# A diffusion layer and a deformable convolution on one core: five edits in the first image's chain, a new order of work, and 11 instead of 8 taps fetched by SyncE

## The reference

```python
x = x + L0(gn(x))      # gn: group norm, 32 groups of 2 channels
x = x + L1(gn(x))

# L0: two gates g, g1 = relu(bn(dwconv3x3(h))), Sobel gradients gx, gy, then 5 steps:
Dx, Dy = 1/(gy*gy/4 + 1), 1/(gx*gx/4 + 1)
D = 1/(1 + 2*Bx + 2*By);  c0 = 1 - 2*Bx - 2*By       # Bx, By = Dx*DT, Dy*DT
for _ in range(5):
    prev = h
    h = D*(c0*h0 - 2*E*h + cm_x*roll(h,1,2) + cp_x*roll(h,-1,2) + cm_y*roll(h,1,3) + cp_y*roll(h,-1,3))
    h = h + D*(2*DT)*x;  h0 = prev
return relu(bn(h))

# L1: deformable 3x3 convolution
offsets_y, offsets_x, mask = split(conv3x3(x, w_offset) + b_offset)   # 9 taps each
sampled = bilinear(x, y0 + offsets_y, x0 + offsets_x) * sigmoid(mask) # 4 corners of each tap
out = einsum(sampled, filt)
```

## Time and profile before

| | |
|---|---|
| median of three runs | 807.94 us (807.9 to 808.3) |
| the profiled execution | 803.14 us, its span 801.3 us |
| PE busy | 669.2 us (84%), mean granted clock 0.904 |
| DVE busy | 539.4 us (67%) |
| ACT busy | 242.2 us (30%) |
| POOL busy | 544.0 us (68%), of it 568 gathers 538.7 us |
| the chain that ended last | POOL 57%, issue 20%, PE 12%, DVE 7% |

### The profile page before, as it was taken

The page is one execution under the profiler, slowest core; times in us unless marked ns, Lnnn a source line. Parts: engine busy times, 40 slices in busy tenths (PEclk is TensorE's granted clock), DMA queues, the critical chain, the costliest instruction groups (busy, mean ns, idle before and its releaser), DMA issues.

```text
span 801.3 us, 15341 instructions
## 1 busy us (share of the span) xinstructions
PE 669.2 (84%) x4616; PEld 589.9 (74%) x4616; DVE 539.4 (67%) x906; ACT 242.2 (30%) x469; POOL 544.0 (68%) x583
## 2 busy tenths in 40 slices
PE   8976888899899988989799987999799987655656
PEld 6865667788788888768689887778778877544545
DVE  5695479778977896578866895778866796322122
ACT  4414421542145213522144313522154213000000
POOL 2000777777777777777777777777777777777774
PEclk9997988999999999999989998999899998555557
DMA  5102333533353433543353435343353335333432
GB/s 167 56 3 55 97 110 109 159 108 115 109 166 109 128 110 112 163 122 109 109 167 114 121 110 167 107 126 108 113 162 114 109 108 167 111 109 108 114 111 72
DMA packets 55146, 92.80 MB, mean 116 GB/s; under 512 B 13384, under 2 KB 35480, under 8 KB 55064
## 3 DMA queue, kind: packets, MB, share of 16 engines
q0 software_dynamic: 27264, 74.49, 31.9%
q1 hardware_dynamic: 27608, 17.20, 7.7%
q10 hardware_dynamic: 192, 0.15, 0.1%
HBM read 79.37 MB, written 12.40 MB: 115 GB/s over the span
## 4 chain that ended last, share of the span: by engine, by line
POOL 57%; issue 20%; PE 12%; DVE 7%; ACT 2%; DMA 1%; POOLq 0%; SPq 0%; DVEq 0%; ACTq 0%
POOL pixels L558 57%; PE banks L1150 9%; PE banks L1153 4%; DVE weighted L903 1%; DMA pixels<-table,index 1%; DVE banks L759 1%; DVE prod L778 0%; DVE prod L798 0%; DVE row_squares L582 0%; ACT coef_T L1051 0%; DVE prod L816 0%; DVE prod L779 0%; ACT sampled_T L1063 0%; DVE banks L760 0%; DMA taps<-taps_in 0%
## 5 line engine op out<-in xcount | busy, mean ns | idle before, releaser
L558 POOL DMA_INDIRECT pixels<-table,index x568 | 538.7, 948 | 247.6 <-issue 172.4
L1153 PE MATMUL banks<-const,weighted 128*128 128x128 f32 x1280 | 194.5, 308 | 62.8 <-DVE weighted L903 49.5
L903 DVE TENSOR_TENSOR weighted<-pixels,banks 128x2304 f32<-128x2304 f32 (+1 forms) x65 | 161.2, 2480 | 115.7 <-DMA pixels<-table,index 111.8
L1153 PEld LDWEIGHTS banks<-const,weighted 128*128 128x128 f32 x1280 | 169.6, 163 | 73.9 <-DVE weighted L903 53.8
L1063 ACT ACTIVATE sampled_T<-banks 128x512 f32<-128x512 f32 (+1 forms) x128 | 55.7, 435 | 335.1 <-PE banks L1153 334.3
L1153 PE MATMUL banks<-const,prod 128*128 128x128 f32 x816 | 109.9, 278 | 19.3 <-DVE prod L778 12.9
L1153 PEld LDWEIGHTS banks<-const,prod 128*128 128x128 f32 x816 | 90.7, 143 | 28.2 <-DVE banks L760 14.1
L1150 PE MATMUL banks<-conv_w,xT 128*128 128x64 f32 (+2 forms) x576 | 97.7, 325 | 0.7 <-ACT banks L1040 0.7
L1150 PEld LDWEIGHTS banks<-conv_w,xT 128*128 128x128 f32 x576 | 91.4, 191 | 7.0 <-ACT banks L1040 1.6
L1150 PE MATMUL banks<-filt,sampled_T 128*128 128x64 f32 x640 | 87.0, 286 | 7.2 <-ACT sampled_T L1063 7.2
L1150 PEld LDWEIGHTS banks<-filt,sampled_T 128*128 128x128 f32 x640 | 81.5, 202 | 13.5 <-ACT sampled_T L1063 11.5
(11 more groups left out here) (144 smaller groups left out, 651.6 us busy)
## 6 DMA issues: line engine op xcount, KB each, us to landing
far_pixels<-table SPq DMA_DIRECT2D x1024, 1.0 KB
pixels<-table,index POOLq DMA_INDIRECT x568, 2.7
table<-xn SPq DMA_DIRECT2D x48, 128.0 KB
table<-xn SPq DMA_DIRECT2D x16, 144.0 KB
x<-x_in SPq DMA_DIRECT2D x30, 64.0 KB, 2.6
out_dram<-x SPq DMA_DIRECT2D x60, 32.0 KB
table<-corner_w SPq DMA_DIRECT2D x16, 70.0 KB
const<-const_in SPq DMA_DIRECT2D x2, 384.0 KB, 3.9
```

The lines of the kernel that those rows point to most:

```text
L558: pool.indirect_dma_start(out=pixels[:, col % NB, k, :], out_offset=None, in_=table[0:(u + 1) * TY * TX, :], in_offset=bass.IndirectOffset ...
L903: return dve.tensor_tensor(weighted[:, col % 2, :, a:b, :].rearrange("p q k c -> p k q c"), entries.rearrange("p k (q c) -> p k q c", c=C) ...
L1153: return pe.matmul(dst, data, moved, start=start, stop=stop, is_transpose=True, skip_group_check=True)
```

## The change

- SyncE fetches 1, 1, 2, 1, 2, 1, 2, 1 taps of the images' last columns (`FAR_TAPS`, 11 in all) instead of one each; GpSimd gathers as many fewer (`gathered`). The addresses are made in bytes on VectorE (`far_addresses`), and the DMA takes them as an offset into the table seen as bytes. The first 32 fetches of an image stand where they stood, the others (96 or 224) in one run in the second half.
- The halo column is made by PE together with the turned edges and copied by VectorE within `edges2`; the table's write waits for that (`emptied(u, "edges2")`).
- The cell below a position is found by adding and subtracting a large constant (`ROUND`): two operations instead of four.
- ScalarE loads its function tables by set; `log` and `exp` share one set.
- In image 0 alone: h's first value is copied to PSUM by ScalarE (`init+0`) instead of being made by PE, into a bank that PE writes once ahead of it; the force of each step is added by PE (`stf1` to `stf4`, four transposes each) instead of VectorE; the gates' differences are split in two (`ownx`, `owny`), and they go to another bank.
- The orders of the three engines are new. At the start VectorE's is now `rows1+0 mean1+0 rows1+1 rowsq1+0 var1+0 bnpa+0 bnpb+0 bnpc+0 scale1+0 shw+0` (before: `rows1+0 mean1+0 bnpa+0 rowsq1+0 bnpb+0 var1+0 bnpc+0 shw+0 scale1+0`, and `rows1+1` after image 0's last step). In the later images the multiply of the fourth column (`mult@11`, `mult@19`, ...) stands behind `scale1` of the image after next instead of behind `rows2`.

```diff
-FAR_W, FAR_K = WS - 1, K2 - 1
-FAR_REGS, FAR_FIRST = 16, 32
-WARM_UP = (6, 4, 6)
+FAR_TAPS = (1, 1, 2, 1, 2, 1, 2, 1)
+FAR_W, FAR_MOST = WS - 1, max(FAR_TAPS)
+FAR_LOADED, FAR_FIRST = 16, 32
+WARM_UP = (6, 1, 6)
...
-rows1+0 mean1+0 bnpa+0 rowsq1+0 bnpb+0 var1+0 bnpc+0 shw+0 scale1+0 dif+0 cells+0 edges1+0 bnout+0 den+0 diff+0
+rows1+0 mean1+0 rows1+1 rowsq1+0 var1+0 bnpa+0 bnpb+0 bnpc+0 scale1+0 shw+0 dif+0 cells+0 edges1+0 bnout+0 den+0
...
             def write_table(u):
-                sp.wait_ge(*emptied(u, "halo"))
+                sp.wait_ge(*emptied(u, "edges2"))
...
-                for p in range(first, last, FAR_REGS):
-                    sp.load(regs, far_index[0:1, u % 2, p:p + FAR_REGS])
-                    for i in range(FAR_REGS):
-                        sp.dma_start(far_pixels[p + i:p + i + 1, u % 2, :], table[bass.ds(sp.snap(regs[i]), 1), :])\
-                          .then_inc(s_far[u], 16)
+                for n in range(first, last, FAR_LOADED):
+                    tap, p = divmod(n, P)
+                    _, at = nc.values_load_multi_w_load_instructions(
+                        far_at[tap:tap + 1, u % 2, p:p + FAR_LOADED], engines=(mybir.EngineType.SP,), min_val=0,
+                        max_val=(ENTRIES - 1) * 4 * ENTRY, skip_runtime_bounds_check_because="positions are clipped")
+                    for i in range(FAR_LOADED):
+                        sp.dma_start(far_pixels[p + i:p + i + 1, u % 2, tap, :].bitcast(u8),
+                                     table_bytes[bass.ds(at[i], 4 * ENTRY)]).then_inc(s_far[u], 16)
...
-                        fetch_far(u + 1, FAR_FIRST, P)
+                        fetch_far(u + 1, FAR_FIRST, FAR_TAPS[u + 1] * P)
...
         def gathered(col):
-            return K2 - 1 if col % WS == FAR_W else K2
+            return K2 - (FAR_TAPS[col // WS] if col % WS == FAR_W else 0)
...
                 for dh in ROW_ORDER:
+                    if what == "edges2" and dh == ROW_ORDER[-1]:
+                        dve.tensor_copy(xn2[:, WS + 1, :], bank(u, what)[:, 2 * P:2 * P + C])
...
                 dve.wait_ge(s_prod, 5 * n)
+                if u == 0:
+
+                    dve.tensor_tensor(target(m), (c0[:, :], c0_T)[1 - m % 2], target(m), ALU.mult).then_inc(s_seeded, 1)
+                    return
...
-                seq(dve.tensor_copy(pos_int[:, :], ps))
-                seq(dve.tensor_copy(lo, pos_int[:, :]))
-                seq(dve.tensor_tensor(ab, lo, ps, ALU.is_gt))
-                seq(dve.tensor_tensor(lo, lo, ab, ALU.subtract))
-                entry = ab[:, 0:WS * K2]
+
+                seq(dve.tensor_scalar(lo, ps, -0.5, ROUND, ALU.add, ALU.add))
+                seq(dve.tensor_scalar(lo, lo, -ROUND, None, ALU.add))
+                entry = entries[:, :]
...
-                    i = len(loaded) % UNUSED
-                    act.activation(unused[:, i:i + 1], one, after)
+                    act.preload_act_table_set(after)
...
+                elif name == "init":
+                    act.wait_ge(s_xn, 1)
+                    act.wait_ge(s_preset_bank, 1)
+                    act.activation(source(0), xn[:, :], ACT.Copy).then_inc(s_init, 1)
...
+            def first_force(m):
+                pe.wait_ge(s_seeded, m)
+                if m % 2:
+                    pe.wait_ge(*emptied(0, "tF"))
+                src = force_T if m % 2 else force[:, :]
+                for j in range(PAIRS):
+                    add(pair(target(m), PAIRS - 1 - j), pair(src, j), eye)
...
-                        mm(bank(0, "conv1"), ones[:, :], x1[0][:, :], True, True).then_inc(s_preset_bank, 1)
+                        for of_engine in (bank(0, "conv1"), source(0)):
+                            ins = mm(of_engine, ones[:, :], x1[0][:, :], True, True)
+                        ins.then_inc(s_preset_bank, 1)
                         warm_up(WARM_UP[1])
```

## The result

The changed kernel takes **849.15 us** (median of four runs, 844.5 to 853.3) against 807.92 of the kernel before: 1.052 times as long, 95% interval 1.049 to 1.055. The prediction was 824.0, with a range of 799 to 845. The direction and the mechanism came as forecast, the size did not: the time lies 4 us above the range.

A forecast was written before the change was run, and what follows sets the result against it. GpSimd's unbroken gathers bound the kernel; SyncE would become the bound at images 3, 5 and 7. Start +2.1, gathers -3.8 and stalls +18 sum to +16.3: 824 us by the median, range 799 to 845 (forecast's own 811 to 850).

The forecast's parts named there:

- The frame: Whole kernel: time is first gather's start, number of gathers and tail, plus GpSimd's standstill for a table or indices, zero before.
- The gathers: GpSimd: 565 gathers instead of 568, 1.253 us each, -3.8 us if GpSimd remains the bound.
- The room: Time from an even image's row numbers to the end of its 70 gathers: 113 us, against 124 us of SyncE's work.
- a lead of 27: Image 2's indices ahead of their first gather: 27 us, today's 19 to 22 with an estimated 6 for the moved multiply.
- the prediction's own formula: Stall at an odd image: SyncE's time to the next table's landing beyond the lead and 70 gathers; 11 us at image 3.
- The prediction's other sum, 43: Stalls at images 3, 5 and 7 if leads stay at today's 19 to 22 us: 16 + 16 + 11 us.
- The start: First gather 2.1 us later: +6.9 up to image 0's normalised x, -4.8 in the rest of its chain.
- a gain of 1.1 us: Image 0's indices come 1.1 us sooner: two index operations go and `turn+1` no longer stands ahead of `off+0`.
- The tail: Behind the last gather: code and cuts unchanged, so it stays at 10.2 us.
- Rival B: SyncE keeps up with a fetch near 0.27 us, the early wait costs as forecast: 806.3 us; chance 0.25.
- C: SyncE keeps up and the early wait for image 1's input costs nothing: 799.8 us; chance 0.15.
- D: SyncE's register operations save nothing, 0.427 us a fetch: each stall 20 us longer, 860 and more; chance 0.06.

The follow-up runs named there:

- another, with the changed kernel's order at that place: Changed kernel, 11 taps, with image 1's row sums moved behind image 0's first edge copies on VectorE: 1.052 of the kernel before, span 838.6 us.
- The old form of the fetch: Changed kernel, 11 taps, fetching by row numbers instead of byte positions, so one register operation more per fetch: 1.175 of the kernel before, span 943.6 us.
- the run without the wait: Changed kernel with image 1's row sums behind image 0's first edge copies: 1.052 of the kernel before with 11 taps, 0.998 with eight.
- eight taps: Changed kernel with SyncE fetching one tap in every image, 8 instead of 11: 1.006 of the kernel before, span 805.2 us.
- one double in image 2, in image 5: Two runs, changed kernel with a second tap in that image alone: image 2 1.036 of the kernel before, image 5 1.008.
- the warm one: Changed kernel with eight taps, image 1's row sums later and 33 unused ones products on PE: 0.991 of the kernel before, median 797.51 us.
- the warm kernel with both orders: The eight-tap kernel with row sums later and unused ones products, plus image 1's turn and first gradient back ahead on PE: 0.992 of the kernel before.

## Why the prediction was wrong in size and right in kind

**The frame held.** Three terms and a fourth, start, number and tail plus stalls, account for the span within 2 us. One fetch was put at 0.34 us and took 0.336; the register operation went, the MOVE stayed. From an even image's indices to the next table were to be 126 us (2 + 124) and were 124.0. The gathers were -3.8, at 1.253 each.

**The room was mis-sized, and this is the error**: +18 was forecast, 42.9 came.
- At image 3: a lead of 27 was assumed. It was 11.2. The 27 starts from image 4's lead of 22 and not from image 2's own 19, and adds 6 for the moved multiply. The 6 came from a row of an image in which that multiply waits for pixels; in the changed kernel none of the eleven multiplies that VectorE makes between 150 and 260 us waits for pixels (the longest wait ahead of one, 5.13 us, is for PE), so the move frees nothing in images 1 and 2. The lead then fell by 8 more, since image 1's chain became 8 us longer. The run that puts PE's work for image 1 back ahead shortens the stall by 5.0, but another, with the changed kernel's order at that place, reached as much, so the shares of order and clock are open. With a lead of 11.2 the prediction's own formula gives 126 - 11.2 - 87.7 = 27 against 24.9: the formula was sound and its input wrong. I had named a lead that I could not read as what spoke against the forecast, and still took it from a row of image 4.
- At images 5 and 7: 6 + 1 were forecast, 10.5 + 7.5 came. The leads of images 4 and 6 were indeed at the 32 that the prediction gave (31.5 both). But the prediction had SyncE begin an even image's fetches as soon as the row numbers are there. Image 4's indices were ready at 434.18, and SyncE, busy with image 3's fetches until 433.6, then with a store, image 4's table and its landing, began at 444.5 with the first register load. Once it has no idle time left, the stall is no longer a matter of leads but of two sums, 188.7 against 176.7 us a pair. The old form of the fetch shows the same: 224.7 a pair.
- The prediction's other sum, 43 "with today's leads", meets the measured 42.9 by luck: its parts are 16, 16 and 11, the measured ones 24.9, 10.5 and 7.5, and with image 2's own lead of 19 the first would have been 19.

**The start** was put at +2.1 and came at +4.2. x was normalised at 16.7 instead of 17.35. The early wait cost 5.1 us (2.9 of waiting, 1.9 of clock and a rest), where 3.6 and 1 had been set for it; the batch-norm steps took 1.85 as forecast (11.24 to 13.09 in the run without the wait). The 2 us missed fit the offsets: `turn+1` no longer ahead of `off+0` was booked as part of a gain of 1.1 us. It was what brought PE to the higher clock; without it the 36 products took 7.72 us instead of 4.91, as in every profile with neither the turn nor ones products ahead of them. The run with the turn ahead has its first gather 2.3 sooner. But the start is no fixed number: four profiled kernels with the same code up to there (changed, eight taps, one double in image 2, in image 5) have their first gather at 84.9, 83.1, 85.7 and 82.7, so +2.0 to +5.0, and the forecast of +2.1 lies at the lower end.

**The tail** was left at 10.2, as its code is unchanged, and took 12.9. The code is the same; the granted clock in it is not (last section).

**Rival B** (SyncE keeps up) and **C** (faster) needed a fetch of 0.27 us or x landing before 8 us; neither was so. **D** had the right sign and too low a price for the same reason as the forecast: it counted three stalls from leads, and not pairs.

## What to carry to other kernels

Before work is moved to an engine with "idle time", add up what that engine's queue does per period, and compare with the period of the engine that it feeds: as long as the sum is smaller, a delay costs only what exceeds the lead, and the lead has to be read at the very image where it is spent; once it is larger, every period costs the difference. A piece of work that looks free to move on TensorE may be what brings its clock up, a wait put into its way may lose it, and a chain of small products behind an idle stretch is priced by rows at both levels. Thirty-three products without a use, placed in waits, were worth more here (0.998 to 0.991) than the new order and all the edits with it (1 to 0.998).

## What the runs showed of the hardware

**The clock in the tail.** The tail's length goes by the granted clock, with its code unchanged. In the profile of the kernel with eight taps and the row sums later, the transposes and the filter products of the last column but one (start, us):

```profile
784.38 3.68 PE L1163 MATMUL banks<-const,weighted 128*128 128x128 f32 x16 [4.61 <-DVE weighted L912]
...
790.28 2.39 PE L1160 MATMUL banks<-filt,sampled_T 128*128 128x64 f32 x10 [0.37 <-ACT sampled_T L1072]
```

And in the warm one:

```profile
779.35 1.92 PE L1163 MATMUL banks<-const,weighted 128*128 128x128 f32 x16
...
783.03 1.33 PE L1160 MATMUL banks<-filt,sampled_T 128*128 128x64 f32 x10 [0.37 <-ACT sampled_T L1072]
```

3.68 and 2.39 us against 1.92 and 1.33; tails of 14.5 and 10.2. Granted clocks of 0.50 and 1.00 over these stretches, so 1.2 and 2.4 GHz. What PE did before: in the one it sat idle for 4.61 us ahead of the first of them, with the clock at 0.50 already, and in the other it worked on products of the ones matrix from 775.4 up to the first of them, with the clock at 0.50 until 779 and at 1.00 from 780. The other profiles lie at these ends or between: tails of 11.3 to 11.4 where the clock rose but fell again, 12.8 to 13.0 where it rose only in the last 6 us. The ones products are neither needed for the short tail nor enough for it: the kernel before and three others have 10.1 to 10.3 without them, and the warm kernel with both orders has 11.3 with them. The Trainium skill, "TensorE: Matmul & The Clock Gate", section "HAM oscillation — how this bites in real kernels", advises, for matrix products with few rows, to do all products of a row tile before waiting for data, so that the array stays warm. No run here rearranged products in that way.

**Instructions, not bytes, are the price of a small register-addressed fetch.** 1 KB each; 0.336 us without the register operation and 111.6 - 13 x 1.23 = 95.6 us for 224, or 0.427, with it. One 44-ns operation on the queue costs 0.09 us a fetch, twice its own length.
